# Registers of a graph kernel's edge stage loaded as packed words, their fields taken out on the sequencers

## What is computed

```python
enh = node_features + 0.1 * query_emb[None, :]
Q = (enh @ Wq + bq).reshape(N, H, D)        # K, V in the same way
mod_k = K[src] + 0.2 * rel_w[edge_relations][:, None, :]
scores = jnp.einsum('ehd,ehd->eh', Q[dst], mod_k) / D ** 0.5
ex = jnp.exp(scores - jax.ops.segment_max(scores, dst, num_segments=N)[dst])
w = ex / jax.ops.segment_sum(ex, dst, num_segments=N)[dst]
agg = jax.ops.segment_sum(w[:, :, None] * V[src], dst, num_segments=N)
```

## Time and profile before

| | |
|---|---|
| three runs, us | 1229.55, 1229.86, 1232.69; median 1229.86 |
| the profiled execution, us | 1231.86, of which the span of its instructions is 1230.0 |
| TensorE matmuls busy | 1034.3 us, 84% of the span |
| VectorE busy | 883.3 us, 72% |
| ScalarE busy | 814.8 us, 66% |
| GpSimd busy | 792.4 us, 64% |

### The profile page before, as it was taken

One profiled execution on the slowest core, in us unless ns is written; L12 is line 12 of the kernel. 1 busy time (PEld: TensorE's weight loads), 2 busy tenths in 40 slices (PEclk: granted clock), 3 DMA queues, 4 the chain that ended last, 5 costly groups with the idle time before them and its releaser, 6 DMA issues. The chain is left out here.

```text
span 1230.0 us, 28148 instructions
## 1 busy us (share of the span) xinstructions
PE 1034.3 (84%) x6923; PEld 773.3 (63%) x6924; DVE 883.3 (72%) x1938; ACT 814.8 (66%) x2770; POOL 792.4 (64%) x851
## 2 busy tenths in 40 slices
PE   5899966888888888888888888877998489999993
PEld 3577743555555555555555555544896378999993
DVE  6788547899999898999999998953886823333331
ACT  3344410388888888888888888864677456666772
POOL 3576747777777777777777777602784346666662
PEclk9899975599999999999999999987997689999997
DMA  8233438887788787878778777772425724443445
GB/s 243 87 122 123 140 108 241 249 240 229 225 226 227 219 231 220 232 219 230 224 219 232 219 228 225 204 238 82 155 87 150 246 64 70 71 67 65 69 68 130
DMA packets 125490, 212.92 MB, mean 173 GB/s; under 512 B 22638, under 2 KB 86058, under 8 KB 125044
## 3 DMA queue, kind: packets, MB, share of 16 engines
q0 software_dynamic: 46336, 132.09, 40.5%
q1 hardware_dynamic: 79028, 79.31, 21.2%
HBM read 180.32 MB, written 34.21 MB: 174 GB/s over the span
## 5 line engine op out<-in xcount | busy, mean ns | idle before, releaser
L685 POOL DMA_INDIRECT KV<-kv,SRC x440 | 459.3, 1044 | 166.9 <-issue 91.2
L694 ACT ACTIVATE KV<-KV,WS 128x65 f32<-128x65 f32 x1452 | 387.1, 338 | 64.5 <-issue 61.8
L801 PE MATMUL ps_o<-KV,PM 128*128 128x260 f32 x880 | 272.2, 405 | 7.2 <-ACT KV L694 4.4
L776 PE MATMUL ps_qe<-Q,PT 128*128 x1320 | 206.9, 291 | 59.1 <-issue 40.8
L776 PEld LDWEIGHTS ps_qe<-Q,PT 128*128 128x128 bf16 x1320 | 123.4, 100 | 124.8 <-issue 89.2
L708 ACT COPY ACC<-ps_o x439 | 157.2, 358 | 32.1 <-PE ps_o L801 24.6
L801 PEld LDWEIGHTS ps_o<-KV,PM 128*128 128x128 f32 x880 | 135.6, 194 | 55.6 <-issue 17.2
L895 DVE TENSOR_TENSOR KV<-KV,ps_qe 128x512 f32<-128x512 f32 x220 | 141.8, 677 | 0.3
L888 DVE TENSOR_TENSOR KV<-KV,ps_u 128x1024 f32<-128x1024 f32 x110 | 132.9, 1208 | 10.1 <-DMA KV<-kv,SRC 9.2
L901 DVE TENSOR_REDUCE S<-KV 128x16 f32<-128x1024 f32 x110 | 132.4, 1204 | 0.9
L1552 POOL DMA_INDIRECT acc<-YG,DX x56 | 88.9, 1587 | 61.0 <-issue 36.6
(11 more groups left out here) (304 smaller groups left out, 1604.3 us busy)
## 6 DMA issues: line engine op xcount, KB each, us to landing
dlb<-dl_rows SPq DMA_DIRECT2D x110, 128.0 KB
tyb<-ty_rows SPq DMA_DIRECT2D x110, 64.0 KB
KV<-kv,SRC POOLq DMA_INDIRECT x440
kv<-kvb SPq DMA_DIRECT2D x25, 258.0 KB, 2.5
xs_rows<-xs SPq DMA_DIRECT2D x25, 256.0 KB, 2.5
KV<-xs_rows SPq DMA_DIRECT2D x10, 640.0 KB, 9.7
Q<-in_f_W_dram SPq DMA_DIRECT2D x8, 512.0 KB, 7.2
KV<-in_f_W_dram SPq DMA_DIRECT2D x8, 512.0 KB, 6.7
```

The costliest lines, as they stand in the source:

```text
L685: pool.indirect_dma_start(kv[:, t % RING, :], None, d["kv"], bass.IndirectOffsetOnAxis(ap=T["SRC"][:, t:t + 1], axis=0)).then_inc(s_g[g % ...
L694: m = a.activation(part, part, ACT.Copy, scale=W[:, t // CB_ % 2, at:at + 1])
L776: m = pe.matmul(T["ps_qe"][:, p % 3, k, :], T["PT"][:, h, (p % 2 * 2 + k) * P:(p % 2 * 2 + k + 1) * P], T["Q3"][:, bass.ds(at[k] + n * C, ...
L801: pe.matmul(ps_o[:, bass.ds(bank, A)], PM[:, g % 2, t % G, :], kv[:, t % RING, C:KVW], start=False, stop=True, skip_group_check=True).then ...
```

## The change

A list no longer holds one finished offset per step. For each group of four steps one word holds the four node blocks in 5 bits each (`query_word`), another the banks and the next banks in 2 bits each (`place_word`); for each two steps a third holds both node blocks with their banks (`copy_word`). TensorE loads one word of `query_word` and one of `place_word` a group, ScalarE one of `copy_word` for two steps, VectorE one of `place_word` for the rescaling. `field` takes a field out by shift and mask and multiplies it by its scale. The next bank comes from the same group's word, so nothing is loaded from the step before a group any more. VectorE's lists are made anew in node tiles 0 and 3 to 5. `rescale` moves behind `place` and the first `multiply`.

```diff
+def load_word(nc, engine, ap):
+    return nc.values_load_multi_w_load_instructions(ap, engines=(engine,), min_val=0, max_val=(1 << 24) - 1,
+                                                    skip_runtime_bounds_check_because="a word packs fields of node blocks and banks")[1][0]
+
+def field(word, low, bits, scale, high):
+    part = (word >> low if low else word) & ((1 << bits) - 1)
+    return part.with_bounds(min_val=0, max_val=high) * scale
...
-                q(v.tensor_scalar(T["qRow"][0:1, :].rearrange("a (p k c) -> a k c p", k=2, c=SC // 2), blocks, float(3 * C), None, ALU.mult))
-                q(v.tensor_scalar(T["aRow"][0:1, :].rearrange("a (p k c) -> a k c p", k=2, c=SC // 2), blocks, float(A), None, ALU.mult))
...
+            def gather_digits(word, row, n, base):
+                digits = row.rearrange("a (g k) -> a g k", k=n)
+                q(v.scalar_tensor_tensor(out=word, in0=digits[:, :, n - 1], scalar=base, in1=digits[:, :, n - 2], op0=ALU.mult, op1=ALU.add))
+                for k in range(n - 3, -1, -1):
+                    q(v.scalar_tensor_tensor(out=word, in0=word, scalar=base, in1=digits[:, :, k], op0=ALU.mult, op1=ALU.add))
...
+                if i == 3:
+                    query_words()
                 if i == 4:
-                    bank_rows()
+                    bank_numbers()
+                if i == 5:
+                    copy_words()
+                    place_words()
...
-            def before(q):
-                return (load_values(nc, mybir.EngineType.Activation, T["aRow"][0:1, q:q + 2], (NT - 1) * A),
-                        load_values(nc, mybir.EngineType.Activation, T["last_bank"][0:1, q:q + 2], 2 * 512))
+            def before(t):
+                i = t // 2
+                word = load_word(nc, mybir.EngineType.Activation, T["copy_word"][0:1, i:i + 1])
+                return ([field(word, 7 * k + 2, 5, A, NT - 1) for k in range(2)], [field(word, 7 * k, 2, 512, RO - 1) for k in range(2)])
...
             def rows(G_):
-                return load_values(nc, mybir.EngineType.PE, T["qRow"][0:1, G * G_:G * G_ + G], (NT - 1) * 3 * C)
-            def banks(name, t, n):
-                return load_values(nc, mybir.EngineType.PE, T[name][0:1, t:t + n], 2 * 512)
+                word = load_word(nc, mybir.EngineType.PE, T["query_word"][0:1, G_:G_ + 1])
+                return [field(word, 5 * k, 5, 3 * C, NT - 1) for k in range(G)]
+            def banks(g):
+                word = load_word(nc, mybir.EngineType.PE, T["place_word"][0:1, g:g + 1])
+                return ([field(word, 4 * k, 2, 512, RO - 1) for k in range(G)], [field(word, 4 * k + 2, 2, 512, RO - 1) for k in range(G)])
...
-                bank = load_values(nc, mybir.EngineType.DVE, T["own_bank"][0:1, t:t + 1], 2 * 512)[0]
+                g = c * CG - 1
+                bank = field(load_word(nc, mybir.EngineType.DVE, T["place_word"][0:1, g:g + 1]), 4 * (G - 1), 2, 512, RO - 1)
...
-                if g > 0 and g % CG == 0:
-                    rescale(g // CG)
                 if summed:
                     place(g)
...
                     weigh(g, *by_vector(g)[0])
+                if g > 0 and g % CG == 0:
+                    rescale(g // CG)
```

More of the change, by code:

```diff
@@ new lines, in bank_numbers @@
+            def bank_numbers():
+                row, third, mine, after = (T[n][0:1, :] for n in ("bRow", "third", "mine", "after"))
+                q(v.tensor_scalar(T["third_i"][0:1, :], row, 43.0, None, ALU.mult))
+                q(v.tensor_scalar(T["third_i"][0:1, :], T["third_i"][0:1, :], 7, None, ALU.logical_shift_right))
+                q(v.tensor_copy(third, T["third_i"][0:1, :]))
+                q(v.scalar_tensor_tensor(out=mine, in0=third, scalar=-3.0, in1=row, op0=ALU.mult, op1=ALU.add))
+                q(v.tensor_scalar(third, mine, 2.0, -3.0, ALU.is_ge, ALU.mult))
+                q(v.scalar_tensor_tensor(out=after, in0=mine, scalar=1.0, in1=third, op0=ALU.add, op1=ALU.add))
@@ new lines, in copy_words @@
+            def copy_words():
+                row, mine, after, ahead = (T[n][0:1, :] for n in ("bRow", "mine", "after", "ahead"))
+                q(v.memset(ahead, 0.0))
+                q(v.tensor_tensor(T["third"][0:1, :], mine, after, ALU.add))
+                q(v.scalar_tensor_tensor(out=ahead[:, 1:NS + 1], in0=row, scalar=4.0, in1=T["third"][0:1, :], op0=ALU.mult, op1=ALU.subtract))
+                q(v.tensor_scalar(ahead[:, 1:NS + 1], ahead[:, 1:NS + 1], 3.0, None, ALU.add))
+                gather_digits(T["word"][0:1, :], ahead, 2, 128.0)
+                q(v.tensor_copy(T["copy_word"][0:1, :], T["word"][0:1, :]))
@@ L330, in constants, with place_words @@
+            def place_words():
+                mine, after, word = T["mine"][0:1, :], T["after"][0:1, :], T["word"][0:1, 0:NG]
+                q(v.scalar_tensor_tensor(out=mine[:, 1:NS], in0=after[:, 0:NS - 1], scalar=4.0, in1=mine[:, 1:NS], op0=ALU.mult, op1=ALU.add))
+                gather_digits(word, mine, G, 16.0)
+                q(v.tensor_copy(T["place_word"][0:1, :], word))
             def constants():
@@ L749, in _ @@
                     weights(c)
-            at, bank = before(NS - 2)
-            copy_sums(NS - 1, at[1], bank[1])
+            at, bank = before(NS)
+            copy_sums(NS - 1, at[0], bank[0])
             a.wait_ge(s_pw, NS)
@@ L838, in _ @@
                 if summed:
-                    own = banks("own_bank", g * G, G)
-                    after = banks("next_bank", max(g * G - 1, 0), G)
-                    shift = 1 if g == 0 else 0
+                    own, after = banks(g)
                 def add(k):
@@ L846, in add @@
                         if t >= 2:
-                            clear(t - 1, after[k - shift])
+                            clear(t - 1, after[k])
                         aggregate(t, own[k])
@@ L1738, in build @@
                    "onesr": ((P, P), F32), "ACC": ((P, (NT + 1) * A), F32), "MB": ((P, 2, P + 4), F32),
-                   "SRC": ((P, NS), I32), "DC": ((P, NS), F32), "qRow": ((1, NS), I32), "aRow": ((1, NS), I32),
-                   "own_bank": ((1, NS), I32), "next_bank": ((1, NS), I32), "last_bank": ((1, NS), I32), "nought": ((P, A), BF16),
+                   "SRC": ((P, NS), I32), "DC": ((P, NS), F32), "query_word": ((1, NG), I32), "place_word": ((1, NG), I32),
+                   "copy_word": ((1, NS // 2 + 1), I32), "nought": ((P, A), BF16),
                    "Q3": ((P, NT * 3 * C), BF16), "rel3": ((P, 3, D), BF16), "iota_t": ((P, 1), F32),
@@ L1756, in build @@
                       "BF": ((P, SC, TE), F32), "BB": ((P, SC, TE), F32), "PEN": ((P, SC, 4, P), BF16), "EL": ((P, 4, SC), F32),
-                      "low": ((P, P), F32), "dl0": ((P, 2), F32), "bRow": ((1, NS), F32), "bThird": ((1, NS), F32)})
+                      "low": ((P, P), F32), "dl0": ((P, 2), F32), "bRow": ((1, NS), F32), "third_i": ((1, NS), I32), "third": ((1, NS), F32), "after": ((1, NS), F32), "ahead": ((1, NS + 2), F32), "mine": ((1, NS), F32), "word": ((1, NS // 2 + 1), F32)})
             psum(ph, {"ps_n": ((P, 2, 2, 512), F32), "ps_mq": ((P, 512), F32), "ps_t": ((P, 512), F32), "ps_gram": ((P, 2, 512), F32)})
```

19 lines of the change are left out of this document (5 added, 14 removed).

## The result

| | before | changed |
|---|---|---|
| time, us, median of four runs each | 1229.7 | 1304.1 |
| ratio to before, 95% interval | | 1.060 (1.058 to 1.062) |
| span of the profiled execution, us | 1230.0 | 1304.4 |
| one group of the edge stage, us | 5.69 | 6.50 |

The forecast was 1269 us in a range of 1238 to 1312: slower it is, but by 74 us where 39 were forecast. A group's time comes from the register loads as before: from the first load of the banks to the last load of the query rows lie 99 groups.

What follows compares the result with a forecast made beforehand. TensorE's sequencer was taken to become the bound: loads saved and fields added give 5.93 us a group, with 0.15 standing 6.08 against 5.69. Over 100 groups +39 us, so 1269 us as a median, range 1238 to 1312.

Steps and rivals of the forecast that it cites:

- What bounds the kernel: Edge stage: TensorE's sequencer, busy 5.0 of 5.70 us a group, becomes the bound with 5.93 us.
- Loads: TensorE: three register loads become two of one word, 1.83 - 0.72 = 1.11 us a group gained.
- Price of an operation: TensorE's fields: 22 register operations a group at 0.090 us each, 1.98 us more.
- C: Rival: at 0.075 to 0.08 us an operation the change is just covered, 1230 us; chance 0.04.
- Third step of the fused operations: TensorE: the multiplication in 12 fused operations adds some 0.005 us each, 0.06 us a group.
- The standing: TensorE's sequencer: of 0.7 us a group standing free, 0.15 stays, as waits for other engines or a full queue.
- Rival D: The 0.7 us of standing remains beside the longer work, or the clock falls: 1324 us as a median; chance 0.10.
- ScalarE at nothing: ScalarE: fewer loads against 7 more register instructions per pair of steps, costed at nothing.
- The last nine groups: Groups without queries: TensorE's fields against loads saved on TensorE and ScalarE, taken as 0, ends -6 and +4 us.
- Rescaling at nothing: VectorE: meeting its 17 waits (20.3 us) one product later costs TensorE nothing and gains nothing.
- Rival B: Fields are free and VectorE sets the pace, so the rescaling's wait of 0.24 us a group is saved: 1206 us; chance 0.08.
- Lists of the first stage: VectorE, first stage: remaking the lists changes the time by 0, ends -3 and +5 us.

Runs made afterwards that it cites:

- pe_lists: Changed kernel with TensorE reading finished offsets from its three lists again, packed words kept on ScalarE and VectorE: 1221.3 us, 0.993 of the kernel before.
- query_list: Changed kernel with only the query columns as finished offsets again, 15 register operations a group on TensorE instead of 22: 1235.3 us, 1.004 of the kernel before.
- next_aligned: Kernel before with the next banks' list one word further on, so its four-word load starts at a multiple of four: 1204.7 us, 0.979.
- act_quad: Kernel before with next banks' list one word further on and ScalarE's two offsets and two banks in one aligned four-word load: 1192.1 us, 0.970.
- rescale_moved: Kernel before with the rescaling alone moved behind the first multiplication: 1230.6 us, 1.000.
- after_back: Changed kernel with only the rescaling put back in its old place ahead of placing: 1306.7 us, 1.063 of the kernel before.
- packed_act_back: Changed kernel with TensorE on finished offsets, next banks' list one word further on, rescaling in its old place: 1193.0 us, 0.970 of the kernel before.

## Why the prediction was half right

**What bounds the kernel: right.** The step on which the forecast stood, that TensorE's sequencer has only 0.7 us a group to spare and becomes the bound, holds in pe_lists, query_list and next_aligned. Busy shares hid it, since a sequencer's instructions count as busy for no engine. The Trainium skill's rule to find the bound by occupancy ("Perfetto Trace Analysis", section "Identifying the Most-Contended Engine") names VectorE for the kernel before; the runs disagree (moving VectorE's wait: 1.000; one load on TensorE: 0.979). The Trainium skill gives TensorE a queue of 64 instructions ("TensorE: Matmul & The Clock Gate", section "Architectural detail: the array is 16× 32×32, not 1× 128×128"). That such a queue hides the fields is an inference from its depth, and it did not hold here: seven operations were worth 0.68 us a group.

**Loads: right.** Two loads of 0.30 us, 0.72 us with what surrounds them, as forecast.

**Price of an operation: 0.090 taken, 0.098 measured.** "I take 0.034 + 0.056 = 0.090": in the weight loads' starts it is 0.09 to 0.10 us, in query_list 0.68 / 7 = 0.098. 22 x 0.098 = 2.16 us instead of 1.98, +0.18 a group. The lower end of the bounds, 0.034, was far off; the upper one, 0.10, was nearly the value, though it was read from rounded starts: to the nanosecond those four operations lie 0.116 us apart on the mean. Two borders of the rivals are off by a little: with the prediction's own terms the sequencer reaches 5.46 us at 0.069 us an operation, not 0.066, and C's 0.075 to 0.08 give 5.60 to 5.71 us. Nothing hung on them.

**Third step of the fused operations: right.** The eight of clearing and adding last 0.0065 us more on the mean, the twelve of the queries 0.0005: 0.06 a group, as taken.

**The standing: mis-sized, the larger error.** "I take 0.15, near the lower end." The sequencer's own work comes to 0.72 + 0.77 + 2.39 + 0.06 + 2.16 = 6.10 us a group, so of 6.50 some 0.40 is standing, 0.25 more than taken; the 0.7 of before was roughly halved, not gone. The reason given was that all three kinds of waits are others being late, and that these keep their speed. The starts of the sequencer's instructions in the two traces show what became of it. Summed over all neighbouring instructions from 300 to 780 us, the time beyond the usual distance of such a pair (the tenth percentile of its kind) is 0.71 us a group before and 0.40 after. In front of the waits for ScalarE's weighted rows it fell from 0.19 to 0.02 us: that part of the reason held. But most of what is left is no wait for a late engine. 0.09 us a group comes from 0.46 us more in one round of each chunk, between the two waits around the relations. In all 14 such rounds of the window, and in no other, three small matmuls of the softmax stand behind the relations, which the sum left out; VectorE's product, for which the second wait stands, had been done for 2.5 us or more each time. The two waits in such a round, then in the next:

```profile
L84 PEldq EVENT_SEMAPHORE  x2: 51/51/51, 523.1 to 523.7; - x2
L84 PEldq EVENT_SEMAPHORE  x2: 51/51/51, 529.8 to 530.0; - x2
```

Another 0.20 us lies, in pieces under 0.16 us, in front of instructions that wait for nothing, and the other 0.11 is spread over the waits; no run took these apart, and their cause stays open. The 7.8 us of TensorE's idle time that the profile puts down to VectorE's query product are no loss of that size: apart from those rounds, the pauses of the sequencer in front of this wait come to 1.3 us. Rival D, in which all of the 0.7 stays, stood at 1324 us, 20 from the 1304 measured, where the forecast is 35 away; the truth lies between the two, and D, at a chance of 0.10, was the nearer.

Together +0.18 + 0.25 = 0.43 us a group, against 6.50 - 6.08 = 0.42. Both values lie inside the bounds that the range was made from (0.085 to 0.10 us an operation, 0 to 0.4 us of standing), both near the upper end; the 6 us gained behind the groups made the miss in the time smaller than it is in a group.

**ScalarE at nothing: right for the stage, with a gain behind it.** The last nine groups were put at 0 with ends of -6 and +4; the stretch that holds them gave -4.4, although one group with queries in it grew. ScalarE's loads pace there, as act_quad against next_aligned shows (37.6 and 47.0 us), and in the changed kernel half of them are gone (pe_lists: 3.8 us in the same place, with none of TensorE's fields; the moved rescaling has a share in it, for in rescale_moved the stretch takes 1.3 us less).

**Rescaling at nothing: right** (rescale_moved, after_back). That its idle time would fall "much below 1.2 us each" is right only in part: 12.4 us in 15 times, 0.83 each. Rival B, which counted on this wait, needs a kernel in which VectorE paces; in those the move took its idle time away and gave TensorE a wait for the rescaling instead.

**Lists of the first stage: right**, 0.2 us.

**Signs.** Operations 22 a group, gaps of 0.2 us in front of clearing and adding, the clock at 1.00: as forecast. Gathers 295 instead of 316 and VectorE at 81% instead of 86% follow from the longer group.

## What to carry to other kernels

Count what an engine's sequencer does alone, per iteration and with what lies between the starts, before trusting a busy share: an engine at 85% by its matmuls can be the bound through loads and register operations. Small register arithmetic on the engine that paces cost about 0.1 us an instruction here, nearly three times what its row shows, so on TensorE a finished offset in a list beats a packed field. On ScalarE one packed word and one list of four words came out alike (packed_act_back and act_quad); only the two short loads were dear. When idle time is removed from an engine and comes up again elsewhere on it, that engine was waiting for another one.

## What was not expected of the hardware

Register loads have a cheap and a dear form. On TensorE one word takes 0.302 us, four from a multiple of four words 0.329, eight from such a place 0.589, four from one word before such a place 1.003; on ScalarE one word takes 0.278, two 0.49 at odd and at even places alike, four from a multiple of four 0.308. All of these fit one reading, which was inferred from them and not tested further: a full, aligned group of four words goes as one piece, and everything else word by word, 0.21 to 0.26 us for each piece after the first. So four aligned words on ScalarE are cheaper than two.
